# Expert weights split in the routing: TensorE takes the rounded part from the whole, and the loads move behind the rows

## The reference

```python
x = layernorm(x)                                     # (4096, 256)
logits = x @ gate_weight.T                           # 8 experts
top_w, top_i = top_k(softmax(logits), 2)             # normalised to sum 1
# experts that are nobody's first choice may be replaced by a similar one
gu = einsum('nh,efh->enf', x, gate_up_proj)          # F = 256, gate and up: 512 columns
hmid = silu(g) * u
y = einsum('enf,ehf->enh', hmid, down_proj)          # 256 columns
out = einsum('ne,enh->nh', combine, y)
x = x + 0.5 * out
```

## Time and profile before

| what | us |
|---|---|
| time, median of 3 runs (1443.74 to 1455.33) | 1443.84 |
| span of the profiled execution, first to last instruction | 1440.9 |
| its own time beside the span | not listed; the median stands 2.9 above the span |
| constants and logits, layer a | 0 to 59.8 |
| routing, layer a | 59.8 to 106.9 |
| experts, layer a | 106.9 to 351 |
| QKV and attention | 351 to 1034 |
| logits, layer b | 1034 to 1097.9 |
| routing, layer b | 1097.9 to 1145 |
| experts, layer b, and the sum | 1145 to 1440.9 |

### The profile page before, as it was taken

How to read it: one execution, slowest core, us unless ns; L and a number is a source line. 1 busy time by engine, 2 the same in 40 slices (tenths; PEclk the granted TensorE clock), 3 DMA queues, 4 the chain that set the end, 5 groups by cost and what they waited for, 6 DMA issues and landing times. The chain is left out here.

```text
span 1440.9 us, 28115 instructions
## 1 busy us (share of the span) xinstructions
PE 1111.1 (77%) x7114; PEld 671.0 (47%) x7117; DVE 853.0 (59%) x2530; ACT 674.2 (47%) x1676; POOL 463.3 (32%) x520
## 2 busy tenths in 40 slices
PE   3458988875786589999899899998694698897840
PEld 2246766664332134444334334443372577676630
DVE  5763333332884688888788788884177533333335
ACT  3513343332455056766666666666454243333320
POOL 3636666653234400000000000000165456665620
PEclk8558999998778589999999999999897599999975
DMA  7502222223586914555544444440273022222238
GB/s 244 182 1 81 82 79 80 83 77 103 179 262 173 167 16 61 78 74 78 73 60 60 61 60 61 72 57 9 84 232 110 19 75 84 80 81 75 76 122 264
DMA packets 130285, 141.06 MB, mean 98 GB/s; under 512 B 46800, under 2 KB 104592, under 8 KB 130192
## 3 DMA queue, kind: packets, MB, share of 16 engines
q1 hardware_dynamic: 116368, 102.24, 31.8%
q0 software_dynamic: 13824, 37.77, 8.3%
HBM read 86.88 MB, written 52.69 MB: 97 GB/s over the span
## 5 line engine op out<-in xcount | busy, mean ns | idle before, releaser
L1407 ACT ACTIVATE t_prob<-t_psS 128x512 f32<-128x512 f32 (+3 forms) x768 | 328.1, 494 | 189.1 <-PE t_psS L1339 155.6
L1427 DVE CUSTOM_DVE_ANT_0 t_psR<-t_psR,all_causal 128x128 f32<-128x128 f32 (+3 forms) x512 | 246.4, 505 | 60.4 <-PE t_psR L1317 52.9
L1317 PE MATMUL t_psR<-stacks_kst,stacks_qst 96*128 96x512 bf16 (+3 forms) x768 | 231.2, 345 | 29.3 <-PEq L886 20.3
L1336 PE MATMUL t_psS<-stacks_qst,stacks_kst 99*128 99x512 bf16 (+3 forms) x768 | 224.0, 329 | 2.7 <-ACT t_prob L1407 2.0
L1431 DVE TENSOR_REDUCE t_maxp<-t_psR 128x1 f32<-128x512 f32 x256 | 176.0, 688 | 21.1 <-PE t_psR L1317 20.3
L1350 PE MATMUL t_psO<-t_prob,t_vst 128*32 128x512 f32 (+3 forms) x1536 | 163.6, 498 | 3.0 <-ACT t_prob L1407 1.1
L1317 PEld LDWEIGHTS t_psR<-stacks_kst,stacks_qst 96*128 96x128 bf16 x768 | 70.1, 98 | 201.0 <-DVE t_maxp L1427 103.1
L1308 POOL COPY t_vst<-stacks_v_rows 128x512 f32<-128x512 f32 x16 | 9.9, 616 | 443.3 <-DMA stacks_v_rows<-v_rows 443.2
L670 PE MATMUL be_psG<-b_w,be_xT 128*128 x432 | 119.8, 413 | 13.0 <-issue 8.6
L670 PE MATMUL ae_psG<-a_w,ae_xT 128*128 x432 | 118.2, 408 | 14.3 <-issue 8.1
L763 DVE TENSOR_TENSOR ae_hid<-ae_sg,ae_psG 128x256 f32<-128x256 f32 x72 | 30.4, 422 | 139.1 <-ACT ae_sg L733 106.8
(11 more groups left out here) (284 smaller groups left out, 1901.1 us busy)
## 6 DMA issues: line engine op xcount, KB each, us to landing
qk_parts<-q_parts SPq DMA_DIRECT2D x32, 384.0 KB, 2.8
stacks_qst<-qk_parts SPq DMA_DIRECT2D x96, 128.0 KB, 4.7
stacks_kst<-qk_parts SPq DMA_DIRECT2D x96, 128.0 KB, 7.4
q_yk<-y_rows SPq DMA_DIRECT2D x16, 512.0 KB, 5.4
s_yk<-y_rows SPq DMA_DIRECT2D x16, 512.0 KB, 5.4
o_rows<-t_orow SPq DMA_DIRECT2D x32, 136.0 KB, 8.8
bl_raw<-o_rows SPq DMA_DIRECT2D x8, 544.0 KB, 4.0
xn_rows<-al_xn SPq DMA_DIRECT2D x8, 512.0 KB, 4.3
```

Source lines behind the costliest of these rows:

```text
L1317: nc.tensor.matmul(psR[bank][:, 0:w], qst[slot][0:KROWS, h, i * P:(i + 1) * P], kst[slot][0:KROWS, h, k0:k0 + w], start=True, stop=True).t ...
L1336: ins = nc.tensor.matmul(ps, kst[k][0:MROWS, h, j * P:(j + 1) * P], qst[k][0:MROWS, h, a:(c + 1) * 512], start=True, stop=a > j * P)
L1407: nc.scalar.activation(prob[j % 2][:, h, a:(c + 1) * 512], psS[n % ST_BANKS][:, a - c * 512:512], ACT.Exp, scale=DK ** -0.5).then_inc(exp_ ...
L1427: ins = nc.vector.tensor_tensor_reduce(psR[bank][:, 0:w], psR[bank][:, 0:w], T.causal[:, 512 - w:512], 1.0, -BIG, ALU.add, ALU.max, maxp[: ...
```

## The change

The expert weights are no longer loaded and split among the chunks of the logits phase. All loads are issued by SyncE behind the last chunk's store, two experts at a time, four DMAs for each pair. All eight experts are split in the routing phase. ScalarE rounds as before. TensorE then forms, for each of four pieces (two halves, 512 and 256 columns), identity times the whole (fp32) plus minus-identity times the rounded part (fp32r) in one PSUM bank, and ScalarE copies the bank to `parts[1]`. POOL takes no part. TensorE's order in the routing is: experts 0 and 1, the count, experts 2 to 4, the ranks, experts 5 to 7, the table. ScalarE's is: round an expert, copy back the one before; the exponential comes behind the fourth such step, the number table behind the sixth; the last copies come after the first two table steps. A constant `minus` is made on POOL, and the semaphores live for the whole program.

```diff
-    def load(self, sp, e, b):
-        hold(sp, self.loaded[b], (e // 2) * 32, self.T)
-        for cols, src in self.sources:
-            sp.dma_start(self.parts[1][:, :, bass.ds(e, 1), cols]..., src[bass.ds(e, 1), :, :]...).then_inc(self.loaded[b], 16)
...
-    def low(self, pool, e):
-        hold(pool, self.high_ready, e + 1, self.T)
...
+    CHUNKS = [(k, cols) for k in range(DC) for cols in (slice(0, 512), slice(512, EW))]
+    def load(self, sp, pair):
+        both = slice(pair * self.PAIR, (pair + 1) * self.PAIR)
         for k in range(DC):
+            for cols, src in self.sources:
+                sp.dma_start(self.parts[1][:, k, both, cols].bitcast(F32),
+                             src[both, k * P:(k + 1) * P, :].rearrange("a p f -> p a f")).then_inc(self.loaded[pair], 16)
+    def high(self, act, e):
+        act.wait_ge(self.loaded[e // self.PAIR], (self.layer + 1) * (16 * DC * len(self.sources)))
+        self.nc.scalar.copy(self.parts[0][:, :, e, :], self.parts[1][:, :, e, :].bitcast(F32)).then_inc(self.high_ready, 1)
+    def difference(self, pe, e, banks):
+        pe.wait_ge(self.high_ready, self.layer * E + e + 1)
+        for n, (k, cols) in enumerate(self.CHUNKS):
+            out = banks[n][:, 0:cols.stop - cols.start]
+            if e:
+                pe.wait_ge(self.low_ready, (self.layer * E + e - 1) * len(self.CHUNKS) + n + 1)
+            self.nc.tensor.matmul(out, self.T.ident[:], self.parts[1][:, k, e, cols].bitcast(F32), start=True, stop=False)
+            self.nc.tensor.matmul(out, self.T.minus[:], self.parts[0][:, k, e, cols], start=False, stop=True).then_inc(self.low_done, 1)
+    def low(self, act, e, banks):
+        for n, (k, cols) in enumerate(self.CHUNKS):
+            act.wait_ge(self.low_done, (self.layer * E + e + 1) * len(self.CHUNKS))
+            self.nc.scalar.copy(self.parts[1][:, k, e, cols], banks[n][:, 0:cols.stop - cols.start]).then_inc(self.low_ready, 1)
...
-                    W.load(sp, c, b)
...
+            for pair in range(E // W.PAIR):
+                W.load(sp, pair)
             for b in range(2):
                 sp.wait_ge(xn_stored[b], 16 * (CH // 2))
...
         @block.scalar
         def _(act):
-            for e in range(E - W.ROUTED, E):
-                W.high(act, e, e % 2)
-            act.wait_ge(gap_ready, 1)
-            nc.scalar.activation(expgap[:], gap[:], ACT.Exp).then_inc(exp_ready, 1)
-            nc.scalar.copy(number16[:], ...).then_inc(exp_ready, 1)
+            for e in range(E):
+                W.high(act, e)
+                if e:
+                    W.low(act, e - 1, ps_w)
+                if e == 3:
+                    act.wait_ge(gap_ready, 1)
+                    nc.scalar.activation(expgap[:], gap[:], ACT.Exp).then_inc(exp_ready, 1)
+                if e == 5:
+                    nc.scalar.copy(number16[:], ...).then_inc(exp_ready, 1)
...
-            table_steps(act, by_lane)
+            table_steps(act, by_lane, lambda: W.low(act, E - 1, ps_w))
...
         @block.tensor
         def _(pe):
+            for e in range(2):
+                W.difference(pe, e, ps_w)
             pe.wait_ge(picked_ready, 1)
             nc.tensor.matmul(ps_count[:, 0:NT * E], T.ones_f[:], ...).then_inc(counted, 1)
+            for e in range(2, 5):
+                W.difference(pe, e, ps_w)
             pe.wait_ge(routed_ready, 1)
...
+            for e in range(5, E):
+                W.difference(pe, e, ps_w)
             pe.wait_ge(hot_ready, 2)
...
+            c.link(g.tensor_scalar(T.minus[:], T.ident[:], -1.0, None, ALU.mult))
```

More of the change, by code:

```diff
@@ L114, with __init__ @@
 class Weights:
-    ROUTED = 2
-    def __init__(self, nc, T, M, gate_up, down):
-        self.nc, self.T = nc, T
+    CHUNKS = [(k, cols) for k in range(DC) for cols in (slice(0, 512), slice(512, EW))]
+    PAIR = 2
+    def __init__(self, nc, T, M, gate_up, down, layer):
+        self.nc, self.T, self.layer = nc, T, layer
         self.sources = ((slice(0, 2 * F), gate_up), (slice(2 * F, EW), down))
         self.parts = [M.sb(f"w{part}", [P, DC, E, EW], F32R) for part in range(2)]
-        self.loaded = [M.sem(f"w_loaded{b}") for b in range(2)]
-        self.high_ready, self.low_ready = M.sem("w_high"), M.sem("w_low")
@@ L127, in whole @@
-    def whole(self, e):
-        return self.parts[1][:, :, bass.ds(e, 1), :].bitcast(F32)
-    def load(self, sp, e, b):
-        hold(sp, self.loaded[b], (e // 2) * 32, self.T)
-        for cols, src in self.sources:
[L134 to L139, removed]
@@ L141, in low @@
-    def low(self, pool, e):
-        hold(pool, self.high_ready, e + 1, self.T)
-        one = bass.ds(e, 1)
-        for k in range(DC):
-            self.nc.gpsimd.tensor_tensor(self.parts[1][:, k, one, :], self.parts[1][:, k, one, :].bitcast(F32),
-                                         self.parts[0][:, k, one, :], ALU.subtract).then_inc(self.low_ready, 1)
+        self.loaded, self.high_ready, self.low_done, self.low_ready = T.w_parts_loaded, T.w_high, T.w_low_done, T.w_low
+    def load(self, sp, pair):
+        both = slice(pair * self.PAIR, (pair + 1) * self.PAIR)
+        for k in range(DC):
+            for cols, src in self.sources:
+                sp.dma_start(self.parts[1][:, k, both, cols].bitcast(F32),
+                             src[both, k * P:(k + 1) * P, :].rearrange("a p f -> p a f")).then_inc(self.loaded[pair], 16)
@@ L234, in step @@
                                                 ALU.mult).then_inc(att_ready, 1)
-                if has(-2) and has(W.ROUTED - 2):
-                    W.low(pool, c - 2)
             steps(pool, step)
@@ L353, in step @@
                     ln.deviation(act, c)
-                if has(-2) and has(W.ROUTED - 2):
-                    W.high(act, c - 2, b)
             steps(act, step)
@@ L393, in phase_route @@
         ps_count, ps_before, ps_total, ps_table = (M.ps(n, [P, 512]) for n in ("ps_count", "ps_before", "ps_total", "ps_table"))
+        ps_w = [M.ps(f"ps_w{n}", [P, 512]) for n in range(len(W.CHUNKS))]
         chain_sem, gap_ready, exp_ready, picked_ready, counted, routed_ready, ranked, hot_ready, col_ready, \
@@ L399, in phase_route, with table_steps @@
         iota_e = T.iota[:, 0:E]
-        def table_steps(eng, body):
+        def table_steps(eng, body, between=None):
             for b in range(2):
                 body(b, b)
+            if between:
+                between()
             with eng.Fori(1, SLOTC // CW // 2) as it:
@@ L410, in _ @@
         def _(act):
[L411 to L416 removed]
+            for e in range(E):
[6 more added lines that the diff above has]
+                if e == 5:
+                    nc.scalar.copy(number16[:], bc(T.iota[:], 2, [P, P, CW])).then_inc(exp_ready, 1)
             def by_lane(r, b):
@@ L531, in by_column @@
                                         ALU.mult).then_inc(col_ready, 1)
-            for e in range(E - W.ROUTED, E):
-                W.low(pool, e)
             table_steps(pool, by_column)
@@ L1554, in program @@
         T.w_loaded, T.gate_loaded = M.sem("w_loaded"), M.sem("gate_loaded")
+        T.w_parts_loaded = [M.sem(f"w_parts_loaded{pair}") for pair in range(E // Weights.PAIR)]
+        T.w_high, T.w_low_done, T.w_low = M.sem("w_high"), M.sem("w_low_done"), M.sem("w_low")
         T.x_loaded = [M.sem(f"x_loaded{i}") for i in range(3)]
@@ L1588, in moe @@
             with ExitStack() as layer:
-                W = Weights(nc, T, Mem(nc, layer, tag), gate_up, down)
+                W = Weights(nc, T, Mem(nc, layer, tag), gate_up, down, "ab".index(tag))
                 phase_logits(nc, T, tag + "l", xs, xn_dram, logits, W, o_rows, *loads)
```

1 line of the change is left out of this document (added).

## The result

| | us |
|---|---|
| predicted | 1472.5 (1454 to 1498) |
| changed kernel, median of 4 | 1489.65 (1486.0 to 1497.98) |
| kernel before, beside it, median of 4 | 1446.3 (1443.74 to 1455.33) |
| ratio, 95% interval | 1.031 [1.028, 1.034] |
| profiled span, before and after | 1440.9, 1490.5 |

The account below looks back on a forecast made before the run. SyncE's issues were taken to hold the phase's end, and the TensorE-ScalarE ring to replace VectorE's chain as routing's bound. Terms: -3.2 + 8.3 + 2 x 11.8 = +28.7 us; 1443.8 + 28.7 = 1472.5 us, range 1454 to 1498.

Parts of the forecast that it names:

- the forecast's own: Whole kernel: 1462 to 1483 us, from the bounds of the issues and 3 us either way for the ring; chance 0.55.
- rival 2: Seam after the logits: the queue paces SyncE, 18.6 us for 12.6 in both layers, +40.7, 1484 us; chance 0.15.
- rival 3: Routing: TensorE's clock stays at the lower level, +46 us more, 1519 us; chance 0.15.
- The bound at the seam: End of logits: SyncE's 16 load issues take 12.6 us before routing; layer a -3.2 us, layer b +8.3 us.
- the chunk pace: Layer a's logits: VectorE's own chain sets 3.8 us a chunk, so the last store starts at 43.0 instead of 54.58.
- Rivals 1: Seam after the logits: the issues cost nothing, the store's landing sets the seam, +10.5, 1454 us; chance 0.10.
- The ring: Routing: TensorE and ScalarE wait for each other, 4.2 to 4.3 us an expert; first table product +11.8 us a layer.
- The clock: Routing: TensorE runs 3.5 us at the lower level, then at the upper one, from the second expert on.
- rival 4: Routing: the identity product runs at half its price, table at about T + 30, +4 a layer, 1457 us; chance 0.05.
- POOL's interference: Routing: four VectorE operations beside POOL lose some 1.0 to 1.5 us each; without POOL comparisons take 0.43 us.
- Layer b's logits: Layer b's logits phase: TensorE bounds it; 0.3 us a chunk won, -1.5 us in all (bounds 0 and -3).
- The experts' phase, attention and the sum unchanged: Stages outside logits, seams and routing: no change in time, 0 us.

Follow-up runs that it names:

- padded kernels: Kernel before with 24 or 96 tiny TensorE products (48 or 192 instructions) added in layer a's routing: 1449.33 us, ratio 1.0064, and 1390.87 us, ratio 1.010.
- mended: Changed kernel with pairs 2 to 4 loaded in the routing phase, copies waiting by piece, and 64 filling TensorE instructions: 1385.35 us, ratio 1.008.
- route_loads: Changed kernel with only the first pair loaded behind the last store, the other three by SyncE within the routing phase: 1404.47 us, ratio 1.022.
- padded kernel: Kernel before with 96 tiny products (192 TensorE instructions) behind the count in layer a's routing: 1390.87 us, ratio 1.010.
- second set: Runs on another chip; there the changed kernel, run again unchanged, took 1416.93 us against 1376.64 for the kernel before, ratio 1.030.

## Why the prediction was right, and which step failed

*The time: partly luck.* 1489.65 lies inside the stated range, 1454 to 1498, but outside the forecast's own, 1462 to 1483. The stated range reached up there to make room for rivals 2 and 3, which did not happen; a cost that no rival named filled that room. The direction and the parts that the change touches were not luck, as follows.

*The bound at the seam: right.* SyncE's issues stood on the path: 16 in 12.5 us (forecast 12.6). Last store at 44.1 (43.0), route start 57.7 (56.6): both 1.1 late, 0.7 of it there at the first chunk (12.29 for 11.60); the chunk pace was the forecast 3.8 (12.29 to 38.97, the starts of chunks 0 and 7). Rivals 1 (issues free) and 2 (18.6 us) fell. Taking three quarters of the issues out took 8.4 us from each seam, which shows the cause, and that the loads couldn't have come for nothing: early they delay row stores, late they delay the ring by 4 us.

*What the Trainium skill's figure doesn't cover.* The 16 issues took 0.47 to 1.15 us each. The Trainium skill, page DMA: Bandwidth & Descriptors, section Anatomy of one DMA — SWDGE (gpsimd) path, gives about 50 ns for the sequencer's dispatch of a DMA that GpSimd issues. These are issued by SyncE, and no run here issues the same loads from GpSimd, so that figure can't be used for the seam.

*The ring: right.* A turn of 4.28 us (4.2 to 4.3); count awaited until T + 11.8 (12.1), ranks until T + 24.9 (25.4), table at T + 37.1 and 36.5 (37.9). The terms over-stated it by 0.8 to 1.4 us. The copy's wait for all four pieces, which I priced but didn't single out, was 1 us a turn (4.28 less 3.27), by the run that took it away.

*The clock: right.* Lower level for expert 0, upper from then on; rival 3 fell, as did rival 4.

*POOL's interference: right.* Comparisons all at 0.42; no gain from it, since VectorE then waited for TensorE. The run with two experts on TensorE collected what this step held: 5.4 us a layer.

*Layer b's logits: too hopeful.* -0.2 for the forecast -1.5, an end (0) of its bounds.

*The step that failed: "The experts' phase, attention and the sum unchanged".* Attention took 21.5 us more. I had asked what the change moves in time and on queues, not what it moves in the program's memory. The runs replace the step by this: added TensorE instructions ahead of the attention shift its loop against the blocks in which code is fetched. In the kernel before, a shift of 0 or 256 instructions gives no pause, 48 gives one a return of the loop, 192 two; 192 in the changed kernel two, 256 none. The cost was 9 and 10.4 us of time in the two padded kernels. In the changed one it was about 12 on one chip (mended is 19.1 us under route_loads, and its two tables begin 2.5 and 4.4 us earlier, which leaves 12.2), or 10.8 from two chips (+40.3 on one, +29.5 with the placement mended on another). Each of these differences can be off by several us, as their intervals show. That leaves +28 to +29.5 for the change itself, against 28.7.

*How many blocks.* The program compiled from each run's kernel shows where the loop lies in TensorE's code; this is a count in the program, not a measurement. The loop has 1718 instructions, the waits and register work among them, or 6.7 blocks of 256, and begins at instruction 3633 in the kernel before. Counted with its waits, the changed kernel moves it by 199, with 64 fillers by 263 (mended 264, route_loads 200), the split of two experts by 49, with its fillers by 257. In the six kernels with a shift of 0, 256, 257, 263 or 264 the loop touches seven blocks, and none pauses; in the seven with 48, 49, 192, 199 or 200 it touches eight, and all pause, with 53 to 55 fetches. The second pause stands near a block's end. In the padded kernel it comes seven products behind the first (675.30 to 676.87), in the changed one, whose loop begins 7 instructions later, four (721.20 to 721.70): in both it is ahead of instruction 3847 of the program, just past a multiple of 256 (3840). With a shift of 48 or 49 that place is over 160 instructions behind the loop's start, and no second pause is seen. What fits all of this, without having been measured by itself: after a return to a block that has gone, the block behind it has gone too, and a loop that comes to that one soon (after 15 and 22 instructions here, not after 165) waits again.

Of the 21.5 us in the first pair of profiles, 15.0 are the pauses. The lower clock behind them accounts for some of the rest: in 727 to 733 a clock of 0.55 for 1.00 takes 0.45 of the work of 6 us, near 2.7 us; behind the second pair, in 834 to 840, it was 0.65, near 2.1 us. What is left, some 2 us, lies within what this stage varies by without pauses (542 to 549 us over the kernels here, pauses deducted), and so do the experts' +2.9 and QKV's -2.0. The 3 us by which the first result's +43 exceeds the second set's +40.3 stay unassigned; the two ratios, 1.031 and 1.030, are the same within their intervals.

*What a rule says of it.* The Trainium skill, page Runtime: NRT & Kernel Launch, section Instruction fetch mechanics, states that code is fetched in blocks of 16 KiB, 256 instructions, and that a taken branch to a block outside the current window of two stalls for the fetch. The traces agree on blocks and stall: the queue moved 0.90 MB in 55 transfers, 16.4 KB each, the pauses stand at the loop's returns, and 256 more instructions bring back the state of none. They don't agree on a window of two for TensorE: a loop over seven blocks returned without a pause in six kernels, and there the measurement decides. The same section calls the crossing of a block mostly hidden. The traces agree inside the loop, where the other crossings of a turn show no pause over 2 us; right behind the return it was not hidden, at 2.5 to 4.3 us for the second pause.

## What to carry to other kernels

Give a fast idle engine work only as deep as the path's own waits: two experts in TensorE's idle time made the routing 5.4 us shorter a layer, eight made it 11 us longer, with nearly the same code (the two experts' copies wait by piece). Issues behind the last store of a phase are on the path at 0.8 us each. And before judging any edit ahead of a long loop, look at the instruction queue's count together with pauses that only "issue" ends: 48 instructions in another phase cost 9 us, and with fillers up to the next 256 the pauses went (ratio 0.9965 became 0.991). The pauses alone are no proof: the experts' phases show some of 2.1 to 2.4 us with "issue" in kernels with 35 or 36 fetches too.

## What the runs showed of the hardware that was not expected

- A loop of one engine can pause 2.5 to 4.3 us at each return, depending only on how many instructions of that engine stand ahead of it in the program; here it paused whenever its 1718 instructions touched eight blocks of 256, and never when they touched seven. 35 to 37 instruction fetches go with none, 53 to 55 with two to four pauses.
- Such a pause has a tail: the granted clock was 0.55 over the 6 us behind one pair of pauses, 0.65 behind the other.
- The same kernel takes 1377 to 1380 us on two chips, 1440 on a third and 1446 in the first result, whose chip the record doesn't name; most of the difference lies in the experts' phases (210 against 239 to 247 us each).
- A 512 KB store issued behind 1.5 MB of loads lands late (7.8 us for 3.6, medians), late enough to stop the engine that fills its buffer (3.29 us in the longest of four waits).
